# Target one-hots kept in HBM for a second layer, and gathers paced by TensorE

## The chip, the cores and the metric

One core of one Trainium2 chip. The metric is the device time of one execution in microseconds (us), the median of several runs. The 8 heads, the edge lists and the node features all live on this one core; nothing is exchanged.

## What is computed

12500 nodes with 128 features, 200000 edges sorted by target node. A graph attention part with eight heads and then one head is followed by two SAGE layers; only the latter are touched here:

```python
def _sage_conv(x, src, dst, Wl, Wr, b):
    msg = x[src]
    agg = segment_sum(msg, dst, num_segments=n)
    cnt = segment_sum(ones, dst, num_segments=n)
    agg = agg / max(cnt, 1.0)[:, None]
    return agg @ Wl.T + x @ Wr.T + b

h = _sage_conv(x, src, dst, Wl0, Wr0, b0)
h = relu(_bn_eval(h, g0, be0, rm0, rv0))
h = _sage_conv(h, src, dst, Wl1, Wr1, b1)
out = layernorm(x + _bn_eval(h, g1, be1, rm1, rv1))
```

Both layers use the same edges, so the same sources and targets.

## The kernel before

The program is written engine by engine, with semaphores and no planner: what stands in an engine's list runs in that order. Phases are separated by a barrier (`phase_end`). Phase 10 is the step loop of the first SAGE layer ("layer one", `layer` = 0), phase 12 that of the second ("layer two", `layer` = 1). Each has 100 steps (`by_step`), one for a chunk k of 125 target nodes. A pass over irregular edges ahead of each loop has next to nothing to do with these inputs.

The edges of a chunk stand in lists made earlier in the kernel. 16 groups of 128 edge slots (`GP`) have sources among the first 8000 nodes, whose features TensorE finds in an SBUF table (`table1`); 7 groups (`TP`) are gathered from HBM. Features are held as three bf16 parts, 384 columns in all. In a step, the engines do the following; "fetch" stands for what the code calls `gather` in `pe_step`:

- SyncE (`sp_step`, lines 890 to 921), for chunk k: load the source list, broadcast to 125 partitions, 4096 B each (L898); the target list, 23 bf16 values for each of 128 partitions (L901); the index list for the gathers (L905), once the gathers of chunk k-2 have landed. Then for chunk k-1 its own node rows (L912, in layer two L914 as well), once VectorE has centred chunk k-3.
- GpSimd (`pool_step`, 648): seven indirect gathers into `h_prow[u]` (L659), once the indices are there and the target matmuls of chunk k-2 are done.
- VectorE (`dve_step`, 1969), in this order: `targets` of chunk t (L1986, and L1990, which compares 23 x 125 bf16 columns into `oh_dst[u]`); `turned` of t-2 (L2010); `sources` of t+1 (L1979); `centre` of t-2 (L2018 and what follows); `combine` of t-1 (L2000 to L2002).
- TensorE (`pe_step`, 1451): four rounds of four target matmuls of chunk t-1 (`segment`, L1498) and four fetch groups of chunk t (L1481, four matmuls each); the turns (L1462) and weight products (L1469 to L1471) of chunk t-2 lie between rounds; seven more target matmuls on the gathered rows end the step.
- ScalarE (`act_step`) evicts each fetch group from PSUM (L1217) and stores the results.

Buffers are double (u = k % 2). One of the two `oh_dst` buffers lies in `stg`, the other in `rows`. What VectorE waits for ahead of `sources` is the landing of both lists (semaphore `h_in["lists"]`, 32 a chunk), with line 1975. SyncE's order within a step and the next is thus: L898, L901, L905, L912 (L914), L898.

## Time and profile before

| | |
|---|---|
| device time, median of three runs | 9318.36 us (9315.79 to 9325.67) |
| span of the profiled execution | 7890.3 us |
| the profiled execution's own time | not recorded apart from the runs above |
| busy in the span: TensorE, VectorE, ScalarE, GpSimd | 69%, 61%, 39%, 65% |
| DMA moved in the span | 647.29 MB, 82 GB/s |
| step loop of layer one | about 5420 to 6590 us |
| step loop of layer two | about 6680 to 7890 us |

The span runs from the first to the last instruction in the trace. In the rows, PE is TensorE, PEld its weight loads, DVE VectorE, ACT ScalarE, POOL GpSimd, SP SyncE; a q behind a name (SPq, DVEq) is that engine's sequencer, which waits and issues DMAs. A row such as `7218.69 0.26 SPq L898 DMA_DIRECT2D rows<-list_src x1` says when an instruction began, how long it took, on which engine and line, and what is written from what. What stands in brackets is the idle time of the engine ahead of it, and what ended that. Tiles are named by the buffer in which they lie: the source one-hots are `rhs`, the target one-hots `stg` or `rows`, the gathered rows `acc`.

### The profile page before, as it was taken

The page shows a single profiled execution, that of the slowest core. Times are in us where ns is not written, and L with a number is a line of the kernel's source. Part 1 is how long each engine was busy: PE and PEld are TensorE (multiplying, and loading weights), DVE is VectorE, ACT ScalarE, POOL GpSimd, SP SyncE. Part 2 cuts the span into 40 slices and gives each one's busy share as a digit, 9 for nine tenths or more (in the row PEclk, how much of TensorE's full clock was granted, in tenths as well). Part 3 has the DMA queues.
Part 4 walks back from the last instruction along what each step waited for, and adds up shares of the span by engine and source line. Part 5 has one row for each costly group of instructions (what it writes and reads, how often), then busy time and mean ns, then how long its engine had stood idle before and what let it go on. Part 6 is the DMA issues. An engine that isn't in the chain of part 4 may idle for free.

```text
span 7890.3 us, 195306 instructions
## 1 busy us (share of the span) xinstructions
PE 5464.8 (69%) x50500; PEld 3952.8 (50%) x50501; DVE 4825.2 (61%) x14588; ACT 3085.2 (39%) x7615; POOL 5124.5 (65%) x4726
## 2 busy tenths in 40 slices
PE   3767677777773746777776777435878874888887
PEld 3655556565651336666666666323444442444444
DVE  7555555555556556666666666575666663555555
ACT  2111111111121135555555555413555552666665
POOL 1776767676740157777777777025887784777777
PEclk9977675656555855555555555567999996999999
DMA  3223232323233532222222222033555553544444
GB/s 122 57 56 77 56 77 56 77 56 77 56 76 125 148 47 52 52 51 51 51 51 51 51 51 51 12 91 95 124 124 125 124 125 92 120 116 118 118 118 107
DMA packets 600102, 647.29 MB, mean 82 GB/s; under 512 B 331121, under 2 KB 490355, under 8 KB 599665
## 3 DMA queue, kind: packets, MB, share of 16 engines
q0 software_dynamic: 190000, 384.58, 23.9%
q1 hardware_dynamic: 338379, 238.04, 10.4%
q10 hardware_dynamic: 71640, 23.81, 1.2%
q8 instruction: 23, 0.38, 0.0%
q14 instruction: 60, 0.48, 0.0%
HBM read 562.39 MB, written 83.23 MB: 82 GB/s over the span
## 4 chain that ended last, share of the span: by engine, by line
DVE 27%; issue 19%; POOL 15%; DMA 14%; PE 13%; DVEq 5%; ACT 3%; SPq 3%; ACTq 1%; POOLq 0%
POOL acc L659 8%; POOL rows L639 7%; DMA acc<-list_dst 7%; PE psa L1407 4%; PE psc L1366 3%; DMA rows<-t_gat,idx 2%; DVE acc L1729 2%; DVE acc L1781 1%; DMA acc<-in_x 1%; DVEq L619 1%; DMA acc<-y_d 1%; DVE acc L1728 1%; ACT ohb L1120 1%; PE psc L1498 1%; DVE s_m L1837 1%
## 5 line engine op out<-in xcount | busy, mean ns | idle before, releaser
L639 POOL DMA_INDIRECT rows<-t_gat,idx x3168 | 3142.8, 992 | 1189.8 <-issue 903.3
L659 POOL DMA_INDIRECT acc<-t_part,acc x1400 | 1826.6, 1305 | 546.6 <-issue 460.2
L1407 PE MATMUL psa<-rhs,rows 128*128 128x176 f32 (+1 forms) x6336 | 1713.1, 431 | 23.2 <-DVEq L1922 12.2
L1217 ACT ACTIVATE acc<-psa 128x384 bf16<-128x384 f32 x3200 | 1290.2, 506 | 884.7 <-PE psa L1481 765.8
L1407 PEld LDWEIGHTS psa<-rhs,rows 128*128 128x128 f32 x6336 | 1497.2, 311 | 132.0 <-DVEq L1922 83.2
L1481 PE MATMUL psa<-den,rhs 125*32 125x384 bf16 x12800 | 785.2, 343 | 191.4 <-ACT acc L1217 149.8
L1128 ACT ACTIVATE wgt<-s_d 128x64 f32<-128x64 f32 (+1 forms) x396 | 93.8, 237 | 1625.5 <-DVE s_d L1838 1610.8
L1122 ACT ACTIVATE oht<-psc 22x1024 bf16<-22x1024 bf16 x402 | 407.3, 1013 | 783.9 <-PE psc L1366 730.4
L1395 PE MATMUL psc<-oh,wgt 128*8 128x22 f32 (+1 forms) x6336 | 290.2, 205 | 552.1 <-ACT wgt L1128 543.8
L1071 ACT ACTIVATE acc<-stg,acc 128x128 bf16<-128x128 f32 x1818 | 552.9, 387 | 198.2 <-issue 116.0
L1481 PEld LDWEIGHTS psa<-den,rhs 125*32 125x32 bf16 x12800 | 285.6, 97 | 641.9 <-ACT acc L1217 412.7
L1366 PE MATMUL psc<-identb,ohb 128*22 128x128 bf16 x3216 | 401.5, 303 | 240.4 <-DVE ohb L1813 173.6
L1395 PEld LDWEIGHTS psc<-oh,wgt 128*8 128x8 f32 (+1 forms) x6336 | 234.2, 95 | 659.8 <-ACT wgt L1128 647.6
L1498 PE MATMUL psc<-acc,stg 128*125 128x384 bf16 x2300 | 481.2, 338 | 87.2 <-DMA acc<-t_part,acc 87.2
L1498 PE MATMUL psc<-acc,rows 128*125 128x384 bf16 x2300 | 496.5, 346 | 27.3 <-DMA acc<-t_part,acc 27.3
L1834 DVE TENSOR_SCALAR pen<-psc 128x8 f32<-128x8 f32 x396 | 66.1, 167 | 692.3 <-DMA rows<-t_gat,idx 508.7
L1855 DVE TENSOR_TENSOR rhs<-oh,wgt 128x352 f32<-128x352 f32 x800 | 419.2, 524 | 88.3 <-DVE acc L1921 7.6
L1979 DVE TENSOR_SCALAR rhs<-rows,node 125x2048 bf16<-125x2048 bf16 x200 | 156.2, 781 | 479.7 <-DMA acc<-list_dst 350.5
L1366 PEld LDWEIGHTS psc<-identb,ohb 128*22 128x22 bf16 x3216 | 293.9, 128 | 298.8 <-DVE ohb L1813 203.1
L1498 PEld LDWEIGHTS psc<-acc,stg 128*125 128x125 bf16 x2300 | 290.5, 138 | 208.5 <-DMA acc<-t_part,acc 108.6
L1498 PEld LDWEIGHTS psc<-acc,rows 128*125 128x125 bf16 x2300 | 300.1, 142 | 151.7 <-issue 48.3
L1990 DVE TENSOR_TENSOR stg<-iota,acc 128x2875 bf16<-128x2875 bf16 x100 | 315.7, 3157 | 23.7 <-DVE acc L1986 23.6
(348 smaller groups left out, 7870.4 us busy)
## 6 DMA issues: line engine op xcount, KB each, us to landing
rows<-list_src SPq DMA_DIRECT2D x200, 500.0 KB
rows<-t_gat,idx POOLq DMA_INDIRECT x3168
acc<-y_d SPq DMA_DIRECT2D x50, 1000.0 KB, 5.0
y_d<-stg SPq DMA_DIRECT2D x100, 250.0 KB, 2.8
acc<-t_part,acc POOLq DMA_INDIRECT x1400
acc<-t_sage SPq DMA_DIRECT2D x300, 62.5 KB
adw<-win_d SPq DMA_DIRECT2D x820, 2.2 KB
adw<-win_d SPq DMA_DIRECT2D x788, 0.4 KB
```

The costliest lines, as they stand in the source:

```text
L639: eng.indirect_dma_start(rows[:, j, 0:spec["width"]], None, spec["table"], bass.IndirectOffsetOnAxis(ap=idx[:, j:j + 1], axis=0)).then_inc ...
L659: eng.indirect_dma_start(h_prow[u][:, t, :], None, t_parts[layer], bass.IndirectOffsetOnAxis(ap=h_idx[u][:, t:t + 1], axis=0)).then_inc(h_ ...
L1071: last = eng.activation(e_pos[:, j, :], iota_p[:, :], ACT.Square, bias=e_p[:, j:j + 1])
L1122: eng.activation(oht[:, :, :], p_oht[0:WIN, :, 0:EP], ACT.Copy).then_inc(oht_sb, 1)
L1217: eng.activation(h_rows[:, g, :], psa[:, g % 4, 0:D3], ACT.Copy).then_inc(hyb["ev"], 1)
L1366: last = eng.transpose(p_oht[0:WIN, j, 0:EP], ohb[:, half, j, :], identb[0:EP, 0:EP])
L1395: last = eng.matmul(p_dens[half][0:hd, (j // 2) * WIN:(j // 2 + 1) * WIN], wgt[:, half, j, 0:hd], oh[:, half, j, :], start=(j % 2 == 0), s ...
L1407: last = eng.matmul(sums(half, q, h), rows[:, slot * TH + j, 0:D], right, start=(j == 2 * q), stop=(j == 2 * q + 1))
L1481: last = eng.matmul(psa[q * SLOTS:(q + 1) * SLOTS, g % 4, 0:D3], oh_src[u][:, g, q * SLOTS:(q + 1) * SLOTS], table1[:, 4 * g + q, :], star ...
L1498: last = eng.matmul(psc[0:NP_, 2 + u, 0:D3], oh_dst[u][:, g, :], rows_g, start=(g == 0), stop=(g == GT - 1))
L1855: eng.tensor_tensor(rhs[:, half, two, 0:h * WIN].rearrange("p t (h j) -> p t h j", h=h), oh[:, half, two, :].unsqueeze(2).to_broadcast([EP ...
L1990: link(tt(oh_dst[u], iota1[:, 0:NP_].unsqueeze(1).to_broadcast([EP, GT, NP_]), h_dstm[:, 0:GT].unsqueeze(2).to_broadcast([EP, GT, NP_]), A ...
```

## The change

In layer one, each step stores its target one-hots, `oh_dst[u]`, 128 x 2875 bf16 = 736 KB, to a new HBM tensor `onehots_d`, on SyncE's queue behind the own-row load. In layer two, `targets` (L1986, L1990) and the load of the target list (L901) are left out; SyncE loads the stored one-hots instead, behind a wait for the target matmuls of chunk k-2, and ahead of the own-row loads. `sources` in layer two waits for the source list alone. VectorE in layer one waits for an earlier store to land before it overwrites the buffer. In both layers gather t (t = 1 to 6) of a chunk waits on GpSimd until TensorE has done 2t fetch groups of that chunk.

```diff
+        onehots_d = dram("onehots_d", (NT, EP, GT * NP_), BF16)
+        oh_moved = [n_msg[f"in{u}"] for u in range(2)]
+        moved_before = [16 * ((NC + 1 - u) // 2) for u in range(2)]
+        def onehots_of(e, k):
+            return onehots_d[ds(e + k, 1), :, :].rearrange("o p n -> p (o n)")
 # pool_step, gathers
                 for t in range(TP):
+                    if t:
+                        eng.wait_ge(hyb["gps"], (e + n0) * GP + (k * GP + 2 * t))
+                        eng.sem_inc(alone, 1)
                     eng.indirect_dma_start(h_prow[u][:, t, :], None, t_parts[layer],
 # sp_step, lists
-                if before:
-                    eng.wait_ge(hyb["ohd"], n + (k - 1))
-                eng.dma_start(h_dst[u][:, 0:GT], list_dst[...]).then_inc(h_in["lists"][u], 16)
+                if not layer:
+                    if before:
+                        eng.wait_ge(hyb["ohd"], n + (k - 1))
+                    eng.dma_start(h_dst[u][:, 0:GT], list_dst[...]).then_inc(h_in["lists"][u], 16)
+            def onehots_in(e, k):
+                u = k % 2
+                if later(e, k):
+                    eng.wait_ge(hyb["seg"], e + (n0 + k - 1))
+                eng.dma_start(oh_dst[u].rearrange("p g n -> p (g n)"), onehots_of(e, k)).then_inc(oh_moved[u], 16)
+            def onehots_out(e, k):
+                u = k % 2
+                eng.wait_ge(hyb["ohd"], e + (k + 1))
+                eng.dma_start(onehots_of(e, k), oh_dst[u].rearrange("p g n -> p (g n)")).then_inc(oh_moved[u], 16)
             def step(e, t):
                 if there(e, t):
                     lists(e, t)
+                    if layer:
+                        onehots_in(e, t)
                 if there(e, t - 1):
                     own(e, t - 1)
+                    if not layer:
+                        onehots_out(e, t - 1)
 # pe_step, segment
                 if g == 0:
-                    eng.wait_ge(hyb["ohd"], n + (k + 1))
+                    if layer:
+                        eng.wait_ge(oh_moved[u], e * 8 + (moved_before[u] + 16 * (NT // 2) + 16 * (k // 2 + 1)))
+                    else:
+                        eng.wait_ge(hyb["ohd"], n + (k + 1))
 # dve_step, sources, targets, step
-                eng.wait_ge(h_in["lists"][u], n * 16 + 32 * (k // 2 + 1))
+                eng.wait_ge(h_in["lists"][u], n0 * 16 + e * 8 + 16 * (k // 2 + 1) if layer else e * 16 + 32 * (k // 2 + 1))
                 if later(e, k):
                     eng.wait_ge(hyb["seg"], n + (k - 1))
+                    eng.wait_ge(oh_moved[u], e * 8 + (moved_before[u] + 16 * (k // 2)))
-                if there(e, t):
+                if there(e, t) and not layer:
                     targets(e, t)
```

SyncE also waits at the end of each loop until all of these DMAs have landed.

## Rows read from the trace of the kernel before

**Rows 1.** Whole core: span in us, mean granted TensorE clock.

```profile
core 0: 7890.3 us, clock 0.709
```

**Rows 2.** Stretch, then busy PE, PEld, DVE, ACT, POOL; clock, DMA share, GB/s.

```profile
5440.00:6600.00 1160.00, 922.83 (x9360) 524.26 (x9358) 729.74 (x1494) 649.95 (x1668) 907.04 (x690) 0.98 0.52 122
6700.00:7860.00 1160.00, 959.76 (x9215) 533.49 (x9215) 678.05 (x1446) 705.96 (x1838) 881.70 (x685) 0.94 0.49 118
```

**Rows 3.** Source one-hots (L1979), layer one, then two: duration, first and last start.

```profile
L1979 DVE TENSOR_SCALAR rhs<-rows,node x97: 752/754/996, 5447.4 to 6556.9; 125x2048 bf16<-125x2048 bf16 x97
...
L1979 DVE TENSOR_SCALAR rhs<-rows,node x96: 752/754/995, 6711.5 to 7847.6; 125x2048 bf16<-125x2048 bf16 x96
```

**Rows 4.** Chain of waits by share of the stretch, layer one, then two.

```profile
by line: POOL acc L659 49.9%; issue 25.7%; DMA acc<-list_dst 6.1%; DMA acc<-t_part,acc 5.1%; DVE stg L1990 1.6%; PE psc L1498 1.6%; SPq L946 1.0%; DVE rows L1990 0.8%; PE psa L1481 0.8%; DVE acc L2034 0.7%; DMA acc<-list_idx 0.7%; DVE acc L
...
by line: DMA acc<-list_dst 42.8%; issue 13.4%; PE psa L1481 4.6%; DVE rows L1990 4.4%; PE psc L1498 4.0%; DVE acc L2021 2.3%; DVE acc L2018 2.2%; DVE stg L1990 2.2%; DVE acc L2019 2.2%; SPq L912 1.9%; SPq L898 1.7%; SPq L914 1.6%; PE psc L1
```

**Rows 5.** SyncE's waits (total us, times, longest), layer one, then two.

```profile
SPq L905 <- DMA acc<-t_part,acc: 875.1, 97, 11.8
...
SPq L912 <- DVEq L2022: 596.6, 94, 11.3
```

**Rows 6.** Layer one, gathers: xcount | busy us, mean ns | idle before, releasers.

```profile
L659 POOL DMA_INDIRECT acc<-t_part,acc x690 | 907.3, 1315 | 228.2 <-issue 223.9 <-DMA acc<-list_idx 3.4 <-PE psc L1498 0.9
```

**Rows 7.** In order of time, layer two: start us, us, what [idle before].

```profile
7202.74 1.35 PE L1498 MATMUL psc<-acc,stg 128*125 128x384 bf16 x7
...
7204.29 0.28 SPq L912 DMA_DIRECT2D acc<-t_sage  x1
...
7214.47 0.83 PE L1481 MATMUL psa<-den,rhs 125*32 125x384 bf16 x16
...
7215.23 1.35 PE L1498 MATMUL psc<-acc,rows 128*125 128x384 bf16 x7
7215.53 0.89 DVE L1979 TENSOR_SCALAR rhs<-rows,node 125x2048 bf16<-125x2048 bf16 x1 [3.46 <-DMA acc<-list_dst]
...
7217.50 0.28 SPq L912 DMA_DIRECT2D acc<-t_sage  x1
...
7218.69 0.26 SPq L898 DMA_DIRECT2D rows<-list_src  x1
...
7226.18 0.75 DVE L1979 TENSOR_SCALAR rhs<-rows,node 125x2048 bf16<-125x2048 bf16 x1 [1.46 <-DMA acc<-list_dst]
```

**Rows 8.** In order of time, one period of layer one.

```profile
6452.77 0.28 DVE L2018 TENSOR_TENSOR acc<-psc,rcnt 125x128 f32<-125x128 f32 x1
...
6453.94 0.28 SPq L912 DMA_DIRECT2D acc<-t_sage  x1
...
6454.43 0.28 SPq L898 DMA_DIRECT2D rows<-list_src  x1
...
6463.10 0.75 DVE L1979 TENSOR_SCALAR rhs<-rows,node 125x2048 bf16<-125x2048 bf16 x1 [1.69 <-DMA acc<-list_dst]
...
6463.77 0.28 DVE L2018 TENSOR_TENSOR acc<-psc,rcnt 125x128 f32<-125x128 f32 x1
```

**Rows 9.** DMA queue, 131.5 to 137 us, L994 stores alone: packets, MB, share.

```profile
q1 hardware_dynamic: 127, 2.39, 102.9%
```

**Rows 10.** The same, 6600 to 6640 us, L1043 loads 125 rows alone.

```profile
q1 hardware_dynamic: 5682, 4.35, 34.4%
```

**Rows 11.** DMA issues of the whole run: last number is us to landing.

```profile
rows<-t_sage,idx POOLq DMA_INDIRECT x32, 2.5
```

**Rows 12.** Waits of layer two; then, in order of time, L1990 beside a gather.

```profile
PEld psc L1469 <- DVE acc L2010: 94.9, 95, 1.4
...
7266.90 3.16 DVE L1990 TENSOR_TENSOR rows<-iota,acc 128x2875 bf16<-128x2875 bf16 x1 [0.18 <-DVE acc L1986]
...
7267.29 3.58 POOL L659 DMA_INDIRECT acc<-t_part,acc  x1 [0.30 <-issue]
```

**Rows 13.** GpSimd in the first pass, where every second gather waits (L637).

```profile
721.55 0.94 POOL L639 DMA_INDIRECT rows<-t_gat,idx  x1 [0.30 <-PE psa L1407]
```

More of the change, by code:

```diff
@@ L898, in lists @@
                 eng.dma_start(h_src[u], list_src[ds(e + k, 1), :].to_broadcast([NP_, EP * GP])).then_inc(h_in["lists"][u], 16)
-                if before:
-                    eng.wait_ge(hyb["ohd"], n + (k - 1))
-                eng.dma_start(h_dst[u][:, 0:GT], list_dst[ds(e + k, 1), :, :].rearrange("o p t -> p (o t)")
-                              ).then_inc(h_in["lists"][u], 16)
+                if not layer:
+                    if before:
+                        eng.wait_ge(hyb["ohd"], n + (k - 1))
+                    eng.dma_start(h_dst[u][:, 0:GT], list_dst[ds(e + k, 1), :, :].rearrange("o p t -> p (o t)")
+                                  ).then_inc(h_in["lists"][u], 16)
                 if before:
@@ L1047, in _ @@
                 by_step(eng, sp_step(eng, layer))
+                for u in range(2):
+                    eng.wait_ge(oh_moved[u], moved_before[u] + (layer + 1) * 16 * (NT // 2))
+                    eng.sem_inc(alone, 1)
                 phase_end(eng, 10 + 2 * layer)
```

## The prediction

> **What bounds the kernel now.** The whole-core row comes first: 7890.3 us of span against a median time of 9318.36 us [rows 1]. The 1428 us between them lie outside the span. I have no separate time of the profiled execution, so I take that difference as fixed, work out a change of the span, and add it to 9318.36. The change touches only the two neighbour phases ("layers"), 100 steps each. In the table by stretch [rows 2] TensorE is busy 80 to 83%, GpSimd 76 to 78%, VectorE 58 to 63%; no engine is full, so shares do not name the bound, and the chain must. The first and last starts of the source one-hots (L1979) give the step: (6556.9 - 5447.4) / 96 = 11.56 us in layer one, (7847.6 - 6711.5) / 95 = 11.96 us in layer two [rows 3].
>
> The chain differs by layer [rows 4]. In layer one half of it is GpSimd's gather instruction (L659) plus "issue"; in layer two 42.8% is the landing of the list loads, 6.1% in layer one. SyncE's own waits say the same: in layer one it waits 875.1 us over 97 steps for landed gathers (L905), in layer two 596.6 us over 94 for the centring on VectorE (L912) [rows 5].
>
> So layer one is bound by GpSimd: seven gathers cost 7 x 1.315 = 9.21 us, plus 228.2 us / 98.6 steps = 2.31 us of gaps, 11.52 us [rows 6]. Layer two is bound by a loop through the list load, which one period shows [rows 7]: source one-hots 7215.53, then the centring, own-row load (L912) 7217.50, next source list (L898) 7218.69, next source one-hots 7226.18. The landing is 7.49 us of it and the rest 3.16. In the period of layer one below the rest is 2.33; layer two has one own-row load more. With 2.9 us for the rest, an estimate between the two, the mean landing is 11.96 - 2.9 = 9.1 us.
>
> The same loop exists in layer one, just under GpSimd: issue 6454.43 to one-hots 6463.10 is 8.67, centring 0.67, and from a centring (6452.77) to the issue of the next source list (6454.43) 1.66; together 11.0 us [rows 8]. Its slack under 11.56 is only 0.56 us. That number decides this case.
>
> **Layer one: the store.** L1990 and L1986 stay. Added per step is one DMA of 128 rows x 5750 B = 736 KB on SyncE's queue, issued after the own-row load and directly ahead of the next source list. Its wait (one-hots made) has long been met, since the list was built before the centring that SyncE has just waited for. VectorE's new wait for an old store to land is met too: that store is more than a step old. The issue costs SyncE about the 0.49 us from L912 to L898 [rows 8]. The queue costs more. No row shows such a store beside gathers. In quiet, a store of 128 partitions filled all 16 DMA engines (2.39 MB in 5.5 us, 102.9% share, 434 GB/s), so 736 KB take 1.7 us of every engine [rows 9]. A load of 125 partitions alone took 34.4% of them, 4.35 MB in 40 us or 109 GB/s, in packets of 768 B [rows 10]; the source list, also 125 partitions, would be 512 KB at that rate, 4.7 us alone, and with about 2.5 us of fixed landing (a lone gather [rows 11]) some 7.2 us, where 8.7 to 9.1 are seen: gathers beside it stretch the transfer to 1.3 to 1.4 times. So the store holds the source list back by 1.7 us (quiet) to 2.4 us (stretched); 3.4 us if the stretch is twofold. SyncE's own 0.5 us runs beside the queue and is inside it. I take 2.1 us. The loop becomes 11.0 + 2.1 = 13.1 us, above GpSimd's 11.52: +1.55 us a step, **+155 us**. Ends: with 1.7 and 3.4 us of queue time 12.7 and 14.4 us, +1.15 and +2.85 us, +115 and +285 us; if the store overtook nothing, 0.
>
> The Trainium skill ("DMA: Bandwidth & Descriptors", "Why a DMA increments its semaphore by 16 and not by 1") says that a hardware-issued DMA uses the largest number of engines up to 16 that divides its outer dimension, 5 for 125 rows and 16 for 128, and the section on queues says that each ring starts its descriptors in order. The trace agrees (34.4% against 102.9% share). By that rule the store lies on just the five rings which the source list needs, so by the rule +155 us stays and rival (b) has no room; were the rings filled in turns, it would be 0.
>
> **Layer two: what leaves.** VectorE loses L1986 and L1990, the latter 3.16 us a step [rows 12]. Neither lies in the list loop, so this alone moves nothing: VectorE will wait longer ahead of L1979, where it already sits idle for 3.46 and 1.46 us [rows 7]. It does end TensorE's wait for L2010, 94.9 us over 95 steps [rows 12], which brings the end of TensorE's step about 0.9 us forward. GpSimd loses its stall: the gather that starts under L1990 takes 3.58 us instead of 0.94 [rows 12, 13], so some 2.6 us a step; while the list loop binds, this is worth little. The small target list (L901) goes; sources then wait only for the source list: I take -0.45 us, an estimate of about one issue on the queue.
>
> [...]
>
> **Layer two: what comes.** A 736 KB load per step on the same queue, behind a wait for the last target matmul (L1498) of two steps back; queued behind that wait are the own-row loads (L912, L914) and the next source list. That matmul ended at 7216.58 where L912 issued at 7217.50, and at 7204.09 where L912 issued at 7204.29 [rows 7]: a lead of 0.2 to 0.9 us, 0.55 in the middle. The load's queue time of 2.1 us plus 0.45 us of issue, less that lead, is 2.0 us on the source list. Here the delay eases itself: each microsecond that the loop grows puts the matmul's end a microsecond further ahead of L912, so half remains, 1.0; TensorE's 0.9 us does the same, -0.45; with it goes the list's 0.45. What is left is about +0.1 by this count, +1.1 if the matmul's end moves along with the loop and nothing eases. I take **+0.5 us, +50 us**; ends -0.5 and +1.5 us (-50, +150 us). The loaded tile itself is needed a step later, and hides.
>
> **The gather waits.** Between gathers GpSimd has a gap of 0.30 us, with a wait and a semaphore increment between them in the first pass too (the gather at 721.55 was released by TensorE [rows 13]), so the instructions cost 0. As waits: twelve fetch groups of a step are done before the last four start (7214.47), 2.1 us before the step's last target matmul (7216.58) [rows 7]. The rows are needed only at the end of the next step; the last gather (0.95 + 2.5 us of landing) has about 9 us left. In layer one GpSimd today runs behind TensorE, so the values have been reached. 0 in both; if the waits trimmed the bursts beside the list load, -0.2 us a step, which I leave to the range.
>
> **Sum.** 9318 + 155 + 50 = **9523 us**.
>
> **Rivals.** (a) *The VectorE lock is what counts (faster).* Store, load and list go through the queues side by side; layer one stays at GpSimd's 11.5 us. In layer two the list loses 0.45 us and, with gathers no longer piled up behind the stall, some of its stretch: 1.35 to 1.2 of 4.7 us is 0.7 us. That is 10.8 us, -1.15 x 100: 9203 us. For it: the rows show the stall, and DMA engines are busy only half of the time [rows 2]. Against: layer two's chain holds hardly any gather, and the queue is where the list waits. 15%. (b) *The new DMAs hide.* The queue time is under the 0.56 us of slack in layer one and eases wholly in layer two: 9300 to 9340 us, 10%. Also where the gather waits never hold and nothing else counts. (c) *Contention doubles.* Store +285 us, and in layer two the wait for L1498 sits behind the longer queue, +150: 9750 us, 15%. It decides where the queue time passes 3 us. (d) *A gather wait takes the place of the stall*: it costs once the last gather lands after the next step's end, 9 us away; as a price 1 us a step, 9620 us with the rest, 3%, inside the range.
>
> **How the numbers follow.** The forecast holds 57%: 9380 to 9640. The range takes in it, (b), (d) and most of (c): 9290 to 9720 us. A measurement of this kernel tells about 0.2% (19 us) from no change. Faster by more: 0.17 ((a) and a little of (b)). Within: 0.08. Slower by more: 0.75.
>
> **What would show it.** In the profile after: L1979 starts 13.1 us apart in layer one, 12.5 in layer two; the source list landing after 10.8 us in layer one; SyncE's wait in layer one moved from L905 to L912; the gather's long instruction gone from layer two but not from one, with its mean near 0.95 us; DMA share in the layers from 0.5 to about 0.6. I am wrong if layer one keeps 11.5 us: then the queue does not order store before list. I am wrong in layer two if its step falls under 11.4 us: then the list loop was fed by the stall.

## The result, and the profile after

The changed kernel took **9340.32 us** (median of 7 runs, 9325.86 to 9346.64) against 9311.37 us for the kernel before (7 runs, 9301.48 to 9325.67) in the same comparison: ratio **1.0026**, 95% interval 1.0016 to 1.0036. It is slower, by 29 us, where the prediction said +205 us (9523). The time lies inside the stated range (9290 to 9720 us), but at the place of its rival (b), not at that of the forecast.

The profiled execution of the changed kernel took 9327.19 us. First the span, then the table by stretch; its stretches are the two gather passes ahead of the layers, then layer one and layer two (columns as in [rows 2]).

```profile
core 0: 9325.6 us, clock 0.668
```

```profile
200.00:2800.00 2600.00, 1497.00 (x12520) 1189.43 (x12520) 1116.85 (x4280) 289.63 (x460) 1461.98 (x1519) 0.60 0.21 50
3480.00:6080.00 2600.00, 1464.61 (x15880) 1302.35 (x15879) 1417.12 (x5503) 1103.27 (x2946) 1503.96 (x1532) 0.50 0.22 41
6620.00:7880.00 1260.00, 999.49 (x9127) 540.22 (x9125) 701.25 (x1441) 656.28 (x1634) 858.81 (x675) 0.92 0.59 166
8040.00:9300.00 1260.00, 1008.95 (x9247) 547.32 (x9245) 356.04 (x1264) 727.72 (x1850) 651.83 (x682) 0.92 0.61 165
```

The source one-hots of the two layers (L2011 now), the chain of waits of each, SyncE's largest waits, and the gather group of each, layer one first:

```profile
L2011 DVE TENSOR_SCALAR rhs<-rows,node x100: 743/753/998, 6599.8 to 7885.4; 125x2048 bf16<-125x2048 bf16 x100
...
L2011 DVE TENSOR_SCALAR rhs<-rows,node x100: 752/754/939, 8017.5 to 9294.7; 125x2048 bf16<-125x2048 bf16 x100
```

```profile
by line: issue 33.0%; DMA acc<-list_dst 11.5%; PE psa L1510 10.2%; PE psc L1530 7.0%; another core or an unknown queue 4.1%; DVE rows L2023 3.9%; DVE stg L2023 3.9%; DMA acc<-t_part,acc 2.2%; ACT acc L1246 2.1%; DVE acc L2067 1.6%; SPq L928
...
by line: issue 28.2%; PE psa L1510 19.9%; PE psc L1530 12.7%; DMA rows<-list_src 12.3%; ACT acc L1246 5.1%; another core or an unknown queue 1.7%; ACT acc L1256 1.7%; PE psc L1491 1.7%; PE psc L1498 1.7%; PE psc L1500 1.5%; ACTq L1258 1.2%;
```

```profile
SPq L934 <- DVEq L2062: 219.8, 32, 10.0
...
SPq L923 <- PE psc L1530: 884.0, 98, 11.6
```

```profile
L669 POOL DMA_INDIRECT acc<-t_part,acc x692 | 883.1, 1276 | 427.9 <-PE psa L1510 198.0 <-issue 165.0 <-remote 26.4
...
L669 POOL DMA_INDIRECT acc<-t_part,acc x696 | 665.7, 956 | 631.7 <-PE psa L1510 240.4 <-issue 159.8 <-PE psc L1530 127.4
```

Three things stand in these lines. The span is 9325.6 us of 9327.19: only **1.6 us lie outside it**, not 1428. The steps are (7885.4 - 6599.8) / 99 = 12.99 us and (9294.7 - 8017.5) / 99 = 12.90 us, close to the 13.1 and 12.5 forecast, although the whole cost was 29 us instead of 205: so the steps of before must have been far longer in this comparison than the 11.56 and 11.96 of [rows 3]. And a name is in the chain that the trace of before did not show, "another core or an unknown queue", on a program of one core; in rows of waits the same thing is called "remote". The profile writes it where a semaphore was updated but no instruction that it knows ended near that time.

**The same program ran at different speeds.** The comparisons below were made on four chips: the kernel before took 7900 to 7910 us on three of them and 9181 us on the fourth. The comparison above had 9311 us. Within one comparison its runs agreed to 0.6%. The trace shown ahead of the prediction (span 7890.3 us) was thus taken at the first speed, the times beside it (9318.36 us) at the second. I call them the 7900 and the 9300 speed (9181 us is counted to the latter); every comparison below is within one chip. Each chip was used for one comparison, so whether the chip or the hour makes the speed is not known.

**How the steps are taken apart.** In each layer, for steps 6 to 94, I took the mean time between the starts of the four instructions that close the list loop of [rows 7, 8]: source list issued (L898; L908 in after) to source one-hots (L1979; L2011), "landing"; one-hots to centring (L2018; L2051); centring to own-row load (L912; L934); and own-row load to the next source list, "queue". They add up to the step, to 0.05 us. The least that one-hots to centring takes is 0.67, and centring to own rows 0.84 in layer one and 1.17 in layer two (their lowest quarter in nearly every run); what is above that is waiting for something that is not in the loop, its **slack**. There is slack in the first column too, which the last one tells: the time from the last update of the lists' semaphore, when the list had landed, to the start of the source one-hots. It is 0.2 us where VectorE stands waiting for the list, and more where VectorE comes late.

| us | landing | to centring | to own rows | queue | step | of the landing, after the list was there |
|---|---|---|---|---|---|---|
| 7900, layer one, before (c3_before) | 8.86 | 0.69 | 1.34 | 0.69 | 11.58 | 0.20 |
| 7900, layer one, after (e7_after) | 9.84 | 0.69 | 0.84 | 1.23 | 12.58 | 0.22 |
| 7900, layer two, before | 9.10 | 0.72 | 1.17 | 1.03 | 11.99 | 0.21 |
| 7900, layer two, after | 9.40 | 0.70 | 1.68 | 1.03 | 12.82 | 0.24 |
| 9181, layer one, before (f1_before) | 9.22 | 1.42 | 0.85 | 1.26 | 12.78 | 2.02 |
| 9181, layer one, after (f2_after) | 9.69 | 0.69 | 0.83 | 1.77 | 13.00 | 0.77 |
| 9181, layer two, before | 9.09 | 1.03 | 1.18 | 1.52 | 12.82 | 0.71 |
| 9181, layer two, after | 9.04 | 0.70 | 1.63 | 1.63 | 13.01 | 0.45 |

### The profile page after: what moved, and what is told of

Same layout as the page of the kernel before. It is cut to its first block, busy times and chain, and to the rows that moved or that the text cites. A ratio compares the mean times of both kernels' runs of the same rounds, so it can differ in the third digit from the quotient of the medians.

```text
span 9325.6 us, 197495 instructions
## 1 busy us (share of the span) xinstructions
PE 5682.7 (61%) x50500; PEld 4031.7 (43%) x50501; DVE 4471.4 (48%) x14388; ACT 3124.2 (34%) x7615; POOL 4799.1 (51%) x4726
## 3 DMA queue, kind: packets, MB, share of 16 engines
q1 hardware_dynamic: 352779, 384.66, 13.1%
## 4 chain that ended last, share of the span: by engine, by line
issue 27%; DVE 22%; another core or an unknown queue 17%; PE 13%; DVEq 9%; DMA 6%; ACT 3%; SPq 2%; ACTq 1%; POOL 0%; POOLq 0%
PE psa L1510 4%; PE psc L1530 3%; DVE acc L1953 2%; DMA rows<-list_src 2%; DMA acc<-list_dst 2%; DVEq L626 1%; DVEq L1914 1%; DVE den L1950 1%; ACT acc L1246 1%; DMA acc<-y_d 1%; DVEq L1918 1%; DVE acc L1760 1%; DVE smax L1871 1%; DMA acc<-in_x 1%
## 5 line engine op out<-in xcount | busy, mean ns | idle before, releaser
L646 POOL DMA_INDIRECT rows<-t_gat,idx x3168 | 3080.8, 972 | 2407.1 <-issue 826.7
L669 POOL DMA_INDIRECT acc<-t_part,acc x1400 | 1562.8, 1116 | 1066.2 <-PE psa L1510 440.5
L1436 PE MATMUL psa<-rhs,rows 128*128 128x176 f32 (+1 forms) x6336 | 1740.6, 435 | 55.8 <-issue 39.4
L1246 ACT ACTIVATE acc<-psa 128x384 bf16<-128x384 f32 x3200 | 1334.8, 504 | 1102.0 <-PE psa L1510 637.0
L1436 PEld LDWEIGHTS psa<-rhs,rows 128*128 128x128 f32 x6336 | 1519.3, 314 | 164.1 <-issue 106.6
L1510 PE MATMUL psa<-den,rhs 125*32 125x384 bf16 x12800 | 892.4, 360 | 506.6 <-ACT acc L1246 321.6
L1407 PE MATMUL psc<-adw,oht 22*128 22x17 bf16 (+1 forms) x9648 | 318.5, 166 | 553.5 <-ACT oht L1151 548.8
L1407 PEld LDWEIGHTS psc<-adw,oht 22*128 22x128 bf16 x9648 | 283.6, 98 | 656.2 <-issue 649.1
L2011 DVE TENSOR_SCALAR rhs<-rows,node 125x2048 bf16<-125x2048 bf16 x200 | 153.0, 765 | 843.3 <-DMA rows<-list_src 364.5
L1530 PE MATMUL psc<-acc,rows 128*125 128x384 bf16 x2300 | 521.0, 359 | 0.5 <-issue 0.3
L1530 PE MATMUL psc<-acc,stg 128*125 128x384 bf16 x2300 | 500.1, 348 | 3.1 <-DMA acc<-t_part,acc 2.5
L1530 PEld LDWEIGHTS psc<-acc,rows 128*125 128x125 bf16 x2300 | 314.5, 148 | 117.9 <-issue 56.0
```

The costliest lines, as they stand in the source:

```text
L646: eng.indirect_dma_start(rows[:, j, 0:spec["width"]], None, spec["table"], bass.IndirectOffsetOnAxis(ap=idx[:, j:j + 1], axis=0)).then_inc ...
L669: eng.indirect_dma_start(h_prow[u][:, t, :], None, t_parts[layer], bass.IndirectOffsetOnAxis(ap=h_idx[u][:, t:t + 1], axis=0)).then_inc(h_ ...
L1246: eng.activation(h_rows[:, g, :], psa[:, g % 4, 0:D3], ACT.Copy).then_inc(hyb["ev"], 1)
L1407: last = eng.matmul(p_adx[0:EP, j * k:(j + 1) * k], oht[:, j, :], adw[:, half, j // 2, r * k:(r + 1) * k], start=(r == 0), stop=(r == 2))
L1436: last = eng.matmul(sums(half, q, h), rows[:, slot * TH + j, 0:D], right, start=(j == 2 * q), stop=(j == 2 * q + 1))
L1510: last = eng.matmul(psa[q * SLOTS:(q + 1) * SLOTS, g % 4, 0:D3], oh_src[u][:, g, q * SLOTS:(q + 1) * SLOTS], table1[:, 4 * g + q, :], star ...
```

## Experiments

**Theory.** The store and the load cost what their place in SyncE's queue costs the source list. **Rivals**: the gather waits cost the time; the traffic costs it wherever it stands; the profile's time and the measured time are 1428 us apart for another reason than a fixed overhead.

### Is the 1428 us a fixed overhead? The kernel before once more

The kernel before, nothing edited.

> The kernel before, unchanged, once more with a profile. The trace of after has a span 1.6 us under its time, while the trace of before that the prediction rests on has 1428 us less than its time. Theory A (the trace of before shows an execution that ran in a faster regime than the timed ones): the span comes out at 9300 to 9320 us, the first attention pass, which the change does not touch, takes about 2700 us as in after and not 2090, and the SAGE steps are longer than 11.56 and 11.96 us, about 12.9 us each, since after has 13.1 and 12.95 and is only 29 us longer. Rival B (the 1428 us lie outside the span and my reading of the steps holds): span about 7890 us, steps 11.5 and 12.0 us. The ratio must be 1.000 either way.

Measured 7902.96 us beside 7909.84 for its twin, ratio 1.0000 (0.9990 to 1.0009); the profiled run took 7894.27 us with a span of 7892.6. So the trace ahead of the prediction was of an execution of some 7892 us, and "outside the span" was never more than 2 us. The first step of the prediction had put a difference between two speeds down to an overhead.

### The parts of the change, one by one, at the 7900 speed

Layer one's store alone; layer two stays as before:

```diff
+                    if not layer:
+                        onehots_out(e, t - 1)
...
+                    if not layer:
+                        eng.wait_ge(oh_moved[u], e * 8 + (moved_before[u] + 16 * (k // 2)))
```

> Layer one stores its target one-hots, layer two is as before, no gather waits. My queue theory (the store of 736 KB holds the source list back by 2.1 us in a loop that has 0.56 us of slack): +115 to +285 us, layer one's step 13.1 us. Rival (in the timed regime layer one is bound by something slower, with slack of 1.5 us or more over the list loop): -10 to +50 us.

Measured 8013.45 us, ratio **1.0144** (1.0129 to 1.0160): +104 us by the two medians, +114 by the ratio. Layer one's step 12.69 us, layer two's 11.99. The store costs in kind what it was forecast to cost, in size two thirds to three quarters of it (+155 forecast).

The gather waits alone, in the kernel before:

```diff
                 for t in range(TP):
+                    if t:
+                        eng.wait_ge(hyb["gps"], (e + n0) * GP + (k * GP + 2 * t))
+                        eng.sem_inc(alone, 1)
```

> The kernel before with the gather waits in both layers and nothing else. My prediction: 0, at most -0.2 us a step, so -40 to +10 us. Rival (the waits cost, since GpSimd starts its next chunk's gathers later and loses its lead): +20 to +100 us. Rival (the waits gain, since bursts of gathers slow the list loads): -50 to -150 us.

Measured 7904.77 us, ratio **0.9995** (0.9986 to 1.0004). The waits cost nothing, as forecast.

The changed kernel without those waits (the same three lines removed from it):

> The changed kernel without the gather waits: store in layer one, load in layer two. If the waits are worth nothing, as I predicted, the time is that of after, 1.003 of before. If they spread the gathers to the good of the list loads, this is slower than after, 1.005 to 1.015. If they cost, it is at 0.99 to 1.00.

Measured 8094.05 us, ratio **1.0236** (1.0222 to 1.0250). Steps of 12.75 and 12.86 us.

On another chip, with the whole change beside its parts, to have all in one comparison (before 7900.16 us there):

> The kernel before once more, as the profile that belongs to the other runs of this call. The same unchanged kernel has taken 9311 us beside after, and 7910 us in the call before this one, so there are at least two speeds at which the same program runs. If this call runs at 7900 us: steps 11.5 and 11.9 us. If it runs at 9300 us, theory A of the first call expects a first pass of 2700 us, steps of 12.8 us in both layers, and a span within 5 us of the time; then the list loop is not what binds layer one, and the waits ahead of it are longer.

> The changed kernel. At 7900 us for before: the queue theory says 1.022 to 1.028 (+175 to +220 us), near the 1.0236 that it had without gather waits, steps 12.75 and 12.9 us. At 9300 us for before: 1.003 again, steps 13.0 and 12.9.

> Layer one stores, layer two as before, no gather waits. At 7900 us: 1.014 as already measured (8013 us). At 9300 us: theory S (what binds layer one there has slack over the list loop, so the store hides) 0.998 to 1.005; rival (the store costs the same 1.2 us a step, and something else in the change, the loss of L1990 in layer two or the gather waits, gives it back) 1.010 to 1.016.

> The changed kernel without gather waits. At 7900 us: 1.024 as already measured. At 9300 us: if the gather waits are what gives the store's cost back there, 1.010 to 1.025; if not, 1.003 like after.

Measured: the kernel before again 0.9996 (0.9985 to 1.0007); **the whole change 1.0228** (1.0214 to 1.0242), 8083.66 us, +184 us; the store alone 1.0127 (1.0110 to 1.0143), 8000.91 us; the change without gather waits 1.0239 (1.0223 to 1.0255), 8095.81 us. So at the speed of the trace on which the forecast was made, the change costs +184 us: 101 us the store (104 to 114 in e1_store_only), the rest the second layer, nothing the waits (with them it is 12 us less, inside the two intervals).

The chain of waits in the two layers of e7_after, and SyncE's largest wait in each:

```profile
by line: DMA acc<-list_dst 46.0%; issue 14.2%; PE psa L1510 6.0%; PE psc L1530 3.9%; DVE acc L2052 2.3%; DVE acc L2051 2.3%; SPq L928 2.1%; DVE acc L2067 2.1%; DVE rows L2023 2.1%; SPq L908 1.9%; SPq L934 1.8%; DVE acc L2069 1.8%; ACTq L126
...
by line: DMA rows<-list_src 43.0%; PE psa L1510 11.7%; PE psc L1530 11.2%; issue 8.5%; ACT acc L1246 1.8%; PE psc L1498 1.8%; ACT acc L1256 1.7%; SPq L934 1.6%; PE psc L1500 1.5%; SPq L923 1.4%; SPq L936 1.4%; DVE acc L2054 1.3%; DVE acc L2
```

```profile
SPq L934 <- DVEq L2062: 803.3, 95, 11.4
...
SPq L923 <- PE psc L1530: 841.1, 97, 11.3
```

In layer one the gather (49.9% in [rows 4]) has left the chain and the list's landing has taken its place, from 6.1 to 46.0%; SyncE's long wait has moved from L905 [rows 5] to the own-row load (now L934). In layer two a line stands in front that was in no row of before: SyncE waits for the last target matmul (L1530) ahead of the new load L923. One period of e7_after's layer one, in order of time:

```profile
6105.07 0.28 SPq L934 DMA_DIRECT2D acc<-t_sage  x1
...
6105.54 0.35 SPq L928 DMA_DIRECT2D onehots_d<-stg  x1
...
6106.49 0.28 SPq L908 DMA_DIRECT2D rows<-list_src  x1
...
6116.08 0.84 DVE L2011 TENSOR_SCALAR rhs<-rows,node 125x2048 bf16<-125x2048 bf16 x1 [3.52 <-DMA acc<-list_dst]
...
6116.84 0.27 DVE L2051 TENSOR_TENSOR acc<-psc,rcnt 125x128 f32<-125x128 f32 x1
...
6117.66 0.28 SPq L934 DMA_DIRECT2D acc<-t_sage  x1
```

Own rows 6105.07, store 6105.54, source list 6106.49: the list is issued 1.42 us after the own-row load, where it was 0.49 us in [rows 8]; it lands 9.59 us after issue, where it was 8.67. Both are the store, and VectorE idles for 3.52 us ahead of L2011.

### Why is the source list so late, and does the queue order cost because of that?

The list is broadcast to 125 partitions. The edit loads it into 128 (three partitions are written and never read), in the kernel before and in the one after:

```diff
-                eng.dma_start(h_src[u], list_src[ds(e + k, 1), :].to_broadcast([NP_, EP * GP])).then_inc(h_in["lists"][u], 16)
+                eng.dma_start(h_src_in[u], list_src[ds(e + k, 1), :].to_broadcast([EP, EP * GP])).then_inc(h_in["lists"][u], 16)
```

> The kernel before, unchanged, as the yardstick of this call. It ran at about 7900 us in two comparisons and at about 9311 us in the one that timed the change. Both theories expect a ratio of 1.000; what is wanted is its trace: if its time is near 9311 us, its steps in the two layers at that speed, which no trace has shown yet. If the speed comes from waits that end late, its passes before the layers will be longer too (the first gather phase 2.7 ms instead of 2.1).

> The kernel before with the source list (L898) loaded into 128 partitions instead of 125; VectorE still reads 125. Layer one stays at 11.5 us a step, since GpSimd sets it; layer two, which the list loop sets at 11.9, falls to 11.5. Time 7900 - 40 = 7860 us, ratio 0.993 to 0.997. Theory B: the landing is the wait in the queue behind the gathers, however many engines serve the list: I to S stays above 8 us and the ratio is 1.000 within 0.001.

> The kernel after with the source list loaded into 128 partitions instead of 125. Theory A (25 packets on each of 5 engines make the list late, and the store ahead of it pushes it past GpSimd's step): the list loop gets 2 to 4 us of slack, so the store's 1.1 us a step in layer one and most of the 0.9 us in layer two are gone: steps 11.5 and 11.5 us, time about 8084 - 105 - 130 = 7850 us, ratio 0.99 to 1.00 against before. Theory B (queue order alone): it stays near 8080 us, ratio 1.02. At the speed of 9311 us A gives 9300 or a little less, B 9340.

Measured (this chip: before 7902.28 us): the control 0.9999 (0.9984 to 1.0015), at the 7900 speed once more; the wide list in before **0.9944** (0.9927 to 0.9961), 7859.05 us; the wide list in after **0.9877** (0.9845 to 0.9908), 7803.36 us. Theory A held in both. The landing fell from 8.7 and 9.1 us to 5.8 and 5.9 in before and to 7.6 and 7.0 in after. In before layer two came down to 11.57 us a step, where layer one already was. In after layer one went back to 11.58 us, and layer two to 11.02, below GpSimd's old 11.5. That fits the stall that is gone there: the mean gather took 970 ns in layer two of e11_wide_after and 1328 ns in its layer one, seven to a step. It is also why the time is better than the 7850 us expected. **With the wide list on both sides the change gains 0.7% (7803.36 over 7859.05); with the narrow list it loses 2.3%**, same code otherwise, both at the 7900 speed. In the chains of layer one and two of e11_wide_after the list's landing (listed under the list that was issued last) is down from 46.0% and 43.0% in e7_after to 3.1% and 28.4%:

```profile
by line: DMA acc<-t_part,acc 25.1%; PE psc L1531 17.3%; issue 17.0%; PE psa L1511 10.8%; POOL acc L670 8.3%; DMA acc<-list_dst 3.1%; DVE rows L2024 2.5%; DVE stg L2024 2.5%; ACT acc L1247 1.1%; ACTq L1262 1.1%; PE psc L1492 1.1%; DVE acc L2
...
by line: DMA rows<-list_src 28.4%; PE psa L1511 15.3%; PE psc L1531 13.3%; issue 11.0%; ACT acc L1247 2.9%; ACT acc L1257 2.4%; PE psc L1499 2.3%; PE psc L1501 2.0%; ACTq L1259 1.7%; PE psc L1492 1.6%; SPq L935 1.6%; SPq L924 1.5%; DVE acc 
```

The Trainium skill ("DMA: Bandwidth & Descriptors", "Why a DMA increments its semaphore by 16 and not by 1") says that a DMA uses the largest number of engines up to 16 that divides its count of rows, which makes 5 for 125 rows and 16 for 128. The run agrees: 3 us of the landing went with three rows more. The traces do not name the engine of a packet.

### What does the load of layer two cost?

The kernel after without store and load, and without the waits for them; TensorE multiplies in layer two by the one-hots that layer one left, and VectorE builds none:

```diff
-                    if layer:
-                        onehots_in(e, t)
...
-                    if not layer:
-                        onehots_out(e, t - 1)
```

> The kernel after without the store of layer one and without the load of layer two: TensorE multiplies layer two by the one-hots that layer one left in SBUF, so the sums of layer two are wrong; all its instructions on TensorE are there. VectorE still builds no target one-hots in layer two, and the target list isn't loaded there. Theory A: all of the change's cost is the traffic of store and load; layer one goes back to 11.52 us a step, layer two falls below before's 11.93 since VectorE's 3.6 us lock over GpSimd and a list load are gone: 11.5 or less. Time 7900 - 50 = 7850 us, 7800 to 7880. Rival: the loss of layer two lies in the new order on the queues (no target list, gathers issued earlier), not in the load: then layer two stays at 12.4 to 12.8 us a step and the time at 7950 to 7990 us.

Measured 7854.98 us, ratio **0.9941** (0.9920 to 0.9961), in the comparison of the runs with the wide list. Layer one 11.57 us a step, layer two **11.49** (before 11.97 there, landing 8.59 instead of 9.08, "to own rows" 1.17). All of the change's cost is the traffic and its place; what leaves layer two is worth -0.48 us a step. All of that lies in the landing. Whether it comes from the small target list that is no longer queued or from gathers that no longer pile up behind L1990 is not shown: both left together. Then the load brings 12.82 - 11.49 = 1.33 us, across two comparisons.

### Why only 29 us at the 9300 speed?

> The kernel before, unchanged. Wanted: its trace at the speed of the official comparison (9311 us), where the change cost 29 us instead of 183. Theory A (waits that end late lengthen every loop): the steps of before are then about 12.8 to 12.9 us in both layers instead of 11.5 and 11.9, with GpSimd no longer the sole bound. Theory B (only the passes ahead of the layers are longer): the steps stay at 11.5 and 11.9, and the layers of after at that speed (13.06 and 12.95 us a step) would have to cost 250 us, which the times exclude. If it runs near 7900 us, it shows neither, and its ratio is 1.000.

> The kernel after, unchanged. At about 7900 us for before: ratio 1.023, as in the comparison with e7_after. At about 9311 us for before: 1.003, as in the official one; Theory A says that its steps are then within 0.3 us of those of before at the same speed.

> The kernel after with the source list on 128 partitions, once more. At about 7900 us for before: ratio 0.988, as in the comparison with e11_wide_after. At about 9311 us for before: if the layers there are bound by the landing of the source list as they are at 7900, the same 100 to 250 us go, ratio 0.975 to 0.99; if late semaphores bound them, the list's slack buys little, ratio 0.99 to 1.00.

The three kernels are those already named, unedited. This comparison fell on a slower chip: before 9180.72 us. Measured: f1_before 0.9997 (0.9987 to 1.0008); **f2_after 1.0029** (1.0016 to 1.0041), 9206.10 us, the result of the first comparison once more; f3_wide_after 1.0001 (0.9986 to 1.0016), 9182.22 us. The parts of the change were not measured singly at this speed. The source one-hots of before (layer one, two), then of after:

```profile
L1979 DVE TENSOR_SCALAR rhs<-rows,node x100: 742/752/832, 6489.5 to 7748.2; 125x2048 bf16<-125x2048 bf16 x100
...
L1979 DVE TENSOR_SCALAR rhs<-rows,node x100: 743/753/943, 7878.3 to 9143.9; 125x2048 bf16<-125x2048 bf16 x100
```

```profile
L2011 DVE TENSOR_SCALAR rhs<-rows,node x100: 745/753/989, 6477.2 to 7758.3; 125x2048 bf16<-125x2048 bf16 x100
...
L2011 DVE TENSOR_SCALAR rhs<-rows,node x100: 752/753/967, 7889.6 to 9172.1; 125x2048 bf16<-125x2048 bf16 x100
```

Layer one went from 1258.7 to 1281.1 us, layer two from 1265.6 to 1282.5: +22 and +17 us. Theory A held: **before's step is already 12.8 us there**, and most of the cost disappears in its slack. The chain of f1_before in layer one and two:

```profile
by line: PE psa L1481 24.5%; PE psc L1498 20.0%; another core or an unknown queue 15.4%; issue 11.2%; ACT acc L1217 5.2%; DVE stg L1990 4.4%; PE psc L1469 3.0%; PE psc L1471 2.7%; DVE rows L1990 1.8%; PE psc L1462 1.5%; PE psc L1470 1.4%; D
...
by line: PE psa L1481 25.5%; issue 18.6%; PE psc L1498 16.8%; ACT acc L1217 7.6%; another core or an unknown queue 4.8%; PE psc L1469 2.8%; DVE rows L1990 2.8%; DMA acc<-list_dst 2.6%; PE psc L1471 2.5%; ACT acc L1227 1.9%; PE psc L1462 1.4
```

Neither the gather nor the list landing (42.8% in [rows 4]) holds a large share: TensorE does, with its fetches (L1481), its target matmuls (L1498) and waits behind it. That these bind the step is read from the chain; no run made them shorter. What lengthens it can be followed in order of time in f1_before:

```profile
7022.06 0.51 PE L1481 MATMUL psa<-den,rhs 125*32 125x384 bf16 x8
...
7024.92 0.49 ACT L1217 ACTIVATE acc<-psa 128x384 bf16<-128x384 f32 x1 [3.07 <-remote]
7025.07 0.29 DVE L2000 COPY acc<-psc 125x128 f32<-125x128 f32 x1 [3.71 <-remote]
...
7025.47 0.89 PE L1481 MATMUL psa<-den,rhs 125*32 125x384 bf16 x8 [2.90 <-ACT acc L1217]
...
7025.85 0.94 POOL L659 DMA_INDIRECT acc<-t_part,acc  x1 [2.04 <-remote]
```

TensorE's fetches are done at 7022.57 by the profile. ScalarE, which evicts them, VectorE and GpSimd, which wait for matmuls ended by then, all start 2.4 to 3.3 us later, within a microsecond of each other, and TensorE then waits 2.90 us for ScalarE. By stretches of one microsecond (columns as above) nothing ran meanwhile but one gather, with TensorE's granted clock at 1.00, the upper level of 2.4 GHz, so it is not the clock:

```profile
7023.00:7024.00 1.00, 0.00 (x0) 0.00 (x0) 0.00 (x0) 0.00 (x0) 0.81 (x1) 1.00 0.68 179
7024.00:7025.00 1.00, 0.00 (x0) 0.00 (x0) 0.00 (x0) 0.08 (x1) 0.00 (x0) 1.00 0.83 188
```

The first gather pass shows it more purely. ScalarE's copy of the one-hots' transposes (L1122), waits of the whole run in f1_before (us in total, times, longest), then of c4_before, where no line with "remote" exists for it:

```profile
ACT oht L1122 <- remote: 1575.0, 263, 11.3
...
DVE pen L1834 <- remote: 892.6, 190, 37.3
...
POOL rows L639 <- remote: 562.1, 309, 3.0
...
ACT oht L1122 <- PE psc L1366: 350.7, 135, 10.8
```

```profile
ACT oht L1122 <- PE psc L1366: 722.5, 350, 21.1
```

At the 7900 speed that copy starts 0.04 us after the transposes' end, in the 5th and the 95th of a hundred cases alike; in f1_before 3.84 us after it on average in the first pass and 2.11 in the second. The transposes (1.03 us for 8) and the copy (1.01 us) last as long in both, and so do the DMA packets (the median of those of 4352 B is 286 ns in the slower trace of after, 289 in e7_after). The last target matmul of a step to VectorE's L2000 is 0.83 us in c4_before and 2.82 in f1_before (layer one). From the first of these copies to the last the first pass takes 2664 us instead of 2110, the second 2634 instead of 2125. The second shows once more that it is not the clock, since the granted clock was 0.50 in that pass in both kernels' traces.

The semaphore events of the traces tell where the delay lies. What waited starts as promptly in f1_before as in c4_before: in both 0.02 us after the update on ScalarE, 0.04 on TensorE, and on VectorE 0.02 in layer one and 0.14 in the first pass, in the median. Updates by ScalarE and VectorE come 0.01 us after their instruction's end in both. Updates by TensorE come 0.01 us after its matmul's end in the first pass of c4_before (0.03 in the 99th of a hundred cases), and 1.9 us after it in f1_before, 6.2 in one of ten. So the other engines do not notice late: the update itself is recorded late, or the matmul ended later than the profile models it.

Nor is TensorE alone. SyncE, its waits long met, needs 2.51 us here from the own-row load to the next source list, where it needed 0.49 in [rows 8]:

```profile
6904.99 0.28 SPq L912 DMA_DIRECT2D acc<-t_sage  x1
...
6907.50 0.02 SPq L898 DMA_DIRECT2D rows<-list_src  x1
```

Of SyncE's instructions without a wait, 84 of 786 in 1000 us of layer one of f1_before begin more than 0.4 us after the one before has ended, and 480 of 2986 in 2000 us of the first pass; in c3_before 0 of 860 and 0 of 3784. In the first pass GpSimd has 259 such pauses (41 in c3_before) and TensorE 36 (0). This is the "queue" of 1.26 us in the table instead of 0.69. What pauses the engines' streams of instructions, and whether TensorE's late updates are of the same cause, stays open.

**What it hides.** In layer one of f1_before VectorE hardly ever waits for the list. Ahead of the source one-hots, in 100 steps, in c3_before, then f1_before, then f2_after (us in total, times):

```profile
  DMA acc<-list_dst: 179.2, 79
...
  DMA acc<-list_dst: 22.3, 19
...
  DMA acc<-list_dst: 217.0, 64
```

In f1_before it comes late instead, since it stands ahead of L2000 for TensorE (the whole run):

```profile
DVE acc L2000 <- remote: 309.8, 95, 14.2
```

The list has landed 7.21 us after its issue there and lies ready for 2.02 us; in f2_after it lands after 8.93 us and lies for 0.77. So the store added 1.72 us to the landing itself and 0.51 to the queue, 2.23 in all. Of that, 1.25 us went into the time in which the list lay ready and 0.74 into the slack ahead of the centring (1.42 over 0.67, 0.02 of it left): 2.23 - 1.99 = +0.24 us, measured +0.22. At 7900 the list lands after 8.65 us before and 9.59 after; the store added 0.94 and 0.54, 1.48 in all, over a slack of 0.5: +1.00 measured. So the store costs the list more at the slower speed, not less, and all that is saved is larger slack: 2.6 us in layer one (1.8 of list lying ready, 0.76 behind the one-hots) instead of 0.5. In layer two the list lands 0.25 us later (8.38 to 8.63 us) and lies ready 0.26 us less; "to own rows" grew by 0.45 us for the wait of the new load (7900: 0.51), the queue by 0.11, and 0.33 us of slack took most of it: +0.19 us. And f3_wide_after lets VectorE have the list 8.07 and 6.23 us after issue and is at before's time, with steps of 12.96 and 12.89 us: it gives back what the change cost and no more, so past that the list does not set the step there. The wide list in the kernel before was not measured at this speed.

## Why the prediction was wrong

**The base (failed).** "The 1428 us between them lie outside the span ... I take that difference as fixed" is the step that failed. A span of 7890 us means an execution of 7892; the 9318 us belong to executions at another speed, in which hand-overs from TensorE and SyncE's own issues take longer (f1_before; its trace is the nearest of before to that speed). What bounds the loop there is not what bounds it in the trace, so a sum made on the trace could not be carried over by adding a constant. At the trace's own speed the same sum gives 7892 + 205 = 8097 us, and 8083.66 us was measured.

**What bounds the kernel (right for the trace only).** Layer one at GpSimd with the list loop 0.56 us under it, layer two at the list loop: e10_wide_before confirms both (layer two gained 0.42 us a step, layer one nothing). At 9181 the loop has some 2.6 us of slack in layer one, and TensorE's chain holds the largest share.

**The store (right in kind, too large).** +1.55 us forecast, +1.00 (e7_after) to +1.15 (e1_store_only over 11.54 of c1_before_again) measured at 7900, +0.22 at 9181. Two errors inside partly cancel: the queue time was put at 2.1 us, and the landing grew by 1.0 to 1.2 only (forecast landing 10.8, measured 9.8); SyncE's issue of the store was put at nothing ("inside it") and cost 0.54 us, since the list is issued that much later. Their sum, 1.5 to 1.7, is at or below the 1.7 us of the lower end. 0.5 to 0.6 us of slack was as forecast, for the trace's speed only. (The prediction's words "just the five rings" are to be read as "those five too": by the rule that it cites there, a store of 128 rows lies on 16.)

**Layer two: what leaves.** The stall of GpSimd ended as forecast: mean gather 955 ns in layer two of e7_after against 1231 in its layer one. The list's share was put at -0.45 us; all that leaves is worth -0.48 (e12_no_load), as much as was forecast for the list alone; how much of it is the end of the lock (the gather held up while L1990 runs) was not separated. **What comes** was counted at 1.0 us, half of 2.0, and is 1.33; the total was put at +0.5 and measured +0.83 at 7900, within the ends. The "half eases itself" was too kind: SyncE waits for L1530 in 97 of the steps of e7_after, where a lead of 0.55 us had been counted on.

**The gather waits (right).** 0.9995 alone, where 1.000 was forecast.

**The signs named beforehand.** SyncE's wait moved as said, the long gather left layer two alone (mean 955 ns) and the DMA share rose to 0.59 and 0.61 (forecast 0.6). The steps of 13.0 and 12.9 us in the trace of after look like a hit for 13.1 and 12.5, and are not one: without a trace of before at the same speed they said nothing of the cost.

**The rivals.** (b), "the new DMAs hide", 10%, is what happened to the time, by a mechanism near to its own: the addition is under or just over the slack. It was weighed on slack from the wrong speed, 0.56 us instead of some 2.6. (a), the VectorE lock, is not what counted, but it fits the gain of 0.7% with the wide list, where layer two falls to 11.02 us; no run took away the lock alone. (c) and (d) did not occur.

## What to carry to other kernels

Compare the profile's span with the measured time before any sum: if they differ by more than a few microseconds, the trace is of an execution at another speed, and its slacks are not those of the measured one; say so and widen towards "hidden". Here the slower speed made layer one's step 1.2 us longer and the list's own landing 1.4 us shorter (8.65 to 7.21). Ask also, of a wait that the loop is said to have, in how many steps it really occurs (79 against 19). A transfer of an awkward row count (125) ahead of which a large one is queued is worth mending before work is moved from an engine to the queues: here 128 instead of 125. After that mend the same change that cost 2.3% gained 0.7%, at the 7900 speed; at 9181 us it left the time of before.

## What the hardware showed that was not expected

- One program of one core, with equal durations of instructions and packets, took 7900 to 7910 us on three chips and 9181 and 9311 us in two other comparisons. In the slow ones TensorE's semaphore updates are recorded up to several us after the modelled end of its last matmul (median 1.9 us in the first pass of f1_before, 0.01 in c4_before), while those who wait start as promptly after the update in both (0.02 us on ScalarE), and SyncE pauses by over 0.4 us between instructions that wait for nothing. Whether the update is late or the matmuls really end later than the trace models them was not settled, nor what makes the speed.
- 125 to 128 destination partitions took 3 us off the landing of a 512 KB list beside gathers (8.7 to 5.8 us).
- A 736 KB store ahead of the list on SyncE's queue cost the list, at 7900, 0.9 to 1.2 us of landing and 0.54 us of issue, where such a store takes 1.7 us in quiet; at 9181 it cost it 1.7 and 0.5 us.
- A gather on GpSimd that starts while VectorE's L1990 runs ends 0.82 us after it in the median (c3_before, 201 cases); one that starts before L1990 does takes its usual 0.95 us (146 cases).
